# Attention row sums: GpSimd adds pairs of probability blocks before the product with ones, and the blocks lie in a ring of five units

## The reference, cut to what matters

```
Q = proj(layernorm(x), Wq, bq); K = proj(ctx, Wk, bk); V = proj(ctx, Wv, bv)
scores = einsum('bhqd,bhkd->bhqk', Q, K) / sqrt(32)
attn   = softmax(scores, axis=-1)                 # exp(s - max) / row sum
out    = einsum('bhqk,bhkd->bhqd', attn, V) @ Wo.T + bo
x = x + tanh(g_xattn) * out
x = x + tanh(g_ffn) * moe_ffn(layernorm(x))       # 8 experts, top 2, capacity 615
```

## Time and profile before

| what | value |
|---|---|
| median of the runs | 1855.63 us (1854.19 to 1856.19) |
| profiled execution | 1856.21 us |
| its span, first to last instruction | 1854.4 us |
| mean granted TensorE clock | 0.972 (1.00 in every batch of attention) |
| period of a batch in attention | 111.0 us |
| busy in one period: TensorE, VectorE, ScalarE, GpSimd | 108.7, 82.2, 56.9, 37.2 us |

### The profile page before, as it was taken

How to read it: one execution, slowest core, us unless ns; L and a number is a source line. 1 busy time by engine, 2 the same in 40 slices (tenths; PEclk the granted TensorE clock), 3 DMA queues, 4 the chain that set the end, 5 groups by cost and what they waited for, 6 DMA issues and landing times.

```text
span 1854.4 us, 29309 instructions
## 1 busy us (share of the span) xinstructions
PE 1735.9 (94%) x10322; PEld 881.9 (48%) x10322; DVE 1078.8 (58%) x2087; ACT 805.9 (43%) x1069; POOL 460.5 (25%) x424
## 2 busy tenths in 40 slices
PE   7999999999999999999814999999999999999996
PEld 4324243242423324243202767666666767676664
DVE  6777867677776777867576634435252625434331
ACT  4553735546364554735431615244252616244330
POOL 2322424223333322421211122112122122111102
PEclk9999999999999999999955999999999999999998
DMA  6333263433425433243122363626354363627301
GB/s 223 102 92 114 75 161 106 99 124 94 136 91 138 134 91 113 80 111 106 36 102 79 96 161 87 173 49 184 78 138 115 99 160 87 175 47 193 74 26 25
DMA packets 234302, 202.83 MB, mean 109 GB/s; under 512 B 141588, under 2 KB 182688, under 8 KB 230152
## 3 DMA queue, kind: packets, MB, share of 16 engines
q1 hardware_dynamic: 193288, 181.72, 33.1%
q0 software_dynamic: 40960, 20.41, 6.3%
HBM read 134.08 MB, written 43.63 MB: 96 GB/s over the span
## 4 chain that ended last, share of the span: by engine, by line
PE 82%; DVE 9%; issue 3%; ACT 3%; POOL 1%; DMA 1%; SPq 0%; DVEq 0%; ACTq 0%; POOLq 0%
PE psum L1548 22%; PE psum L1525 21%; PE psum L1353 7%; PE psum L1344 6%; PE psum L1360 6%; PE psum L1334 5%; PE psum L1324 5%; PE psum L1440 4%; PE psum L1371 3%; DVE mx L925 2%; ACT osum L792 1%; DVE reached L1076 1%; DVE x2hl L996 1%; DVE x2hl L998 1%; DVE stats L877 1%
## 5 line engine op out<-in xcount | busy, mean ns | idle before, releaser
L1548 PE MATMUL psum<-w,hT 128*123 128x512 f16 x1920 | 415.7, 379 | 0.0
L1525 PE MATMUL psum<-xgT,w 128*128 128x369 f16 (+1 forms) x3072 | 411.0, 295 | 0.8 <-DVE xgT L1177 0.8
L925 DVE TENSOR_REDUCE mx<-psum 128x1 f32<-128x512 f32 x512 | 331.2, 684 | 109.7 <-PE psum L1334 108.0
L1525 PEld LDWEIGHTS psum<-xgT,w 128*128 128x128 f16 x3072 | 298.2, 97 | 109.9 <-issue 1.9
L1548 PEld LDWEIGHTS psum<-w,hT 128*123 128x123 f16 x1920 | 259.9, 135 | 153.4
L778 ACT ACTIVATE pt<-psum 128x1024 f32<-128x1024 f32 x256 | 260.8, 1022 | 144.3 <-PE psum L1344 144.2
L851 ACT ACTIVATE h<-psum,b1c 128x369 f32<-128x369 f32 (+1 forms) x256 | 117.8, 511 | 331.6 <-PE psum L1525 331.3
L1198 DVE TENSOR_TENSOR hT<-h,hT 128x615 f16<-128x615 f32 x128 | 102.5, 801 | 212.4 <-ACT hT L854 212.4
L671 POOL DMA_INDIRECT out_dram<-y,idx_now x40 | 99.9, 2498 | 481.2 <-DVE y L1230 252.6
L1227 DVE SCALAR_TENSOR_TENSOR y<-psum,b2b 123x512 f32<-123x512 f32 x40 | 27.7, 692 | 269.5 <-PE psum L1548 269.5
L1324 PE MATMUL psum<-actT,wT 128*128 128x512 f16 x768 | 177.6, 379 | 2.0 <-DVE wT L912 2.0
(11 more groups left out here) (187 smaller groups left out, 1503.6 us busy)
## 6 DMA issues: line engine op xcount, KB each, us to landing
stage<-in_L_ffn_W_dram SPq DMA_DIRECT2D x62, 1024.0 KB, 5.3
stk<-qk_rows SPq DMA_DIRECT2D x192, 128.0 KB, 2.6
qk_rows<-qks SPq DMA_DIRECT2D x64, 256.0 KB, 2.5
xin<-in_x_dram SPq DMA_DIRECT2D x8, 1024.0 KB, 5.4
cin<-in_ctx_dram SPq DMA_DIRECT2D x8, 1024.0 KB, 7.5
xres<-in_x_dram SPq DMA_DIRECT2D x8, 1024.0 KB, 5.5
out_dram<-xres SPq DMA_DIRECT2D x32, 256.0 KB, 2.1
x_split<-x2hl SPq DMA_DIRECT2D x32, 256.0 KB, 2.3
```

Of the source, the lines that this page charges most:

```text
L925: v.reduce_max(mx[:, KT * t + qt:KT * t + qt + 1], ps, AX.X).then_inc(read, 1)
L1525: mm = t_.matmul(psum[:, (2 * m + ch) % 4, 0:(c1 - c0) * CP], w1[:, wp, kt, m * P:(m + 1) * P], xgT[:, c0:c1, KT * xp + kt, 0:CP], start=( ...
L1548: mm = t_.matmul(psum[0:CP, Y_BANK[c], :], hT[:, hp, k, c * CP:(c + 1) * CP], w2[:, wp, k, :], start=(k == 0 and (hp, wp) == (0, 0)), stop ...
```

## The change

- **Pairs on GpSimd.** The units 2p and 2p + 1 for p = 0 to 4 are added on GpSimd, in place into the first, four operations of 128x512 f32 a pair: 20 a batch. Before the pairs 0, 2 and 4 GpSimd waits for `mrow_ready` of VectorE's slots 8, 12 and 16.
- **11 products with ones.** `with_ones` now takes a term from a table: pair 0 in slot 10, pair 1 in 12, pair 2 in 14, pair 3 in 16, unit 10 in 17, unit 11 and pair 4 in 18, units 12 to 15 in 19 to 22. Slots 7, 8, 9, 11, 13 and 15 have none. A new semaphore `sums_done` counts them; `pv_done` now counts the products with values.
- **Ring of five.** `pt_units`: two units in `pt`, the other three lie over `qk32`, `x2nT` and `x2n`, which are free at that time. The exponential of unit u waits for the product with ones that used unit u - 5, and the first five for the whole of the batch before and for all of `qk_split`.
- **Two copies.** The activation of 128x1024 becomes one for bank 6 (slots 10, 14, 18) and one for bank 7 (`sums_ready`; slots 12, 16, 18).
- **Later reciprocals.** They move to the slots (15, 16, 16, 17), (17, 18, 18, 19), (19, 20, 20, 21), and `GROUP_NORM` with them from 14, 17, 20, 23 to 17, 19, 21, 23.
- **Norm of the next x.** The four `xin` operations move from GpSimd (L592) to VectorE, slots 5, 5, 6, 6. GpSimd's rstd for them moves ahead of its last two `qks` operations.

```
+PAIRS, PT_UNITS = 5, 5
+SUMS = {10: (("pair", 0),), 12: (("pair", 1),), 14: (("pair", 2),), 16: (("pair", 3),), 17: (("unit", 10),),
+        18: (("unit", 11), ("pair", 4)), 19: (("unit", 12),), 20: (("unit", 13),), 21: (("unit", 14),), 22: (("unit", 15),)}
-RECIP_SLOT = ((11, 12, 13, 14), (15, 16, 16, 17), (19, 19, 20, 20), (23, 23, 23, 23))
+RECIP_SLOT = ((15, 16, 16, 17), (17, 18, 18, 19), (19, 20, 20, 21), (23, 23, 23, 23))
+X_NORM_SLOT = (5, 5, 6, 6)
...
 # GpSimd
+                        if not last:
+                            for tt in range(KT - 1):
+                                inverse_deviation(0, tt, KT * b + (KT + tt))
                         pool.wait_ge(mrow_ready, NG * b + 1)
+                    if i == QK_FIRST + 3 and not last:
+                        inverse_deviation(0, KT - 1, KT * b + (2 * KT - 1))
...
-                pool.wait_ge(mrow_ready, NG * b + 2)
-                if not last:
-                    for tt in range(KT):
-                        ...
-                        g.tensor_scalar(xn[:, tt, :], xin[:, tt, :], mv[:, 0, tt, 0:1], rstd[:, 0, tt:tt + 1],
-                                        ALU.subtract, ALU.mult).then_inc(xn_ready, 1)
-                pool.wait_ge(mrow_ready, NG * b + 3)
+                for p in range(PAIRS):
+                    if p % 2 == 0:
+                        pool.wait_ge(mrow_ready, NG * b + (p // 2 + 2))
+                    pool.wait_ge(pv_done, UNITS * b + (2 * p + 1))
+                    for hf in range(2):
+                        copied(pool, use, ("ST", 2 * p + 1, hf), b)
+                        for j in range(2):
+                            into = pt_units[2 * p % PT_UNITS][:, hf, j, :]
+                            g.tensor_tensor(into, into, pt_units[(2 * p + 1) % PT_UNITS][:, hf, j, :],
+                                            ALU.add).then_inc(pair_added, 1)
                 pool.wait_ge(xres_in, 16 * b + 16)
...
 # ScalarE
-                            act.wait_ge(pv_done, UNITS * b + max(u - 1, 0))
+                            if u < PT_UNITS:
+                                act.wait_ge(sums_done, SUM_COUNT * b)
+                                act.wait_ge(qk_split, NQ * b + NQ)
+                            else:
+                                act.wait_ge(sums_done, SUM_COUNT * b + (sum_of_unit(u - PT_UNITS) + 1))
...
-                        s.activation(osum[:, gr % 2, :, :], psum[:, 6:8, :], ACT.Copy).then_inc(osum_ready, 1)
+                        s.activation(osum[:, gr % 2, 0, :], psum[:, 6, :], ACT.Copy).then_inc(osum_ready, 1)
+                    if t in SUMS_END[:-1]:
+                        gr = SUMS_END.index(t)
+                        act.wait_ge(sums_done, SUM_COUNT * b + (GROUP_SUMS[gr][-1] + 1))
+                        act.wait_ge(norm_done, NG * b + max(gr - 1, 0))
+                        s.activation(osum[:, gr % 2, 1, :], psum[:, 7, :], ACT.Copy).then_inc(sums_ready, 1)
...
 # VectorE
+                        for tt in range(KT):
+                            if t == X_NORM_SLOT[tt]:
+                                normalise(0, tt, KT * b + (KT + tt), xin[:, tt, :], xn[:, tt, :], xn_ready)
...
 # TensorE
+                def with_ones(s):
+                    for kind, n in SUMS.get(s, ()):
+                        i = SUM_ORDER.index((kind, n))
+                        terms = next(t for t in GROUP_SUMS if i in t)
+                        gr = GROUP_SUMS.index(terms)
+                        if i == terms[0] and gr > 0:
+                            pe.wait_ge(sums_ready, (NG - 1) * b + gr)
+                        if kind == "pair":
+                            pe.wait_ge(pair_added, 4 * PAIRS * b + (4 * n + 4))
+                        src = pt_units[(2 * n if kind == "pair" else n) % PT_UNITS]
                         for j in range(4):
-                            last = t_.matmul(psum[32 * j:32 * j + 32, 7, :], ones32[:, :],
-                                             pt[:, (2 * u + j // 2) % 4, j % 2, :], start=(kt == 0), stop=(kt == KT - 1))
-                        last.then_inc(pv_done, 1)
+                            last = t_.matmul(psum[32 * j:32 * j + 32, 7, :], ones32[:, :], src[:, j // 2, j % 2, :],
+                                             start=(i == terms[0]), stop=(i == terms[-1]))
+                        last.then_inc(sums_done, 1)
```

More of the change, by code:

```diff
@@ L51 @@
 GROUP_END = [LAG_C + 4 * g + 3 for g in range(NG)]
-RECIP_SLOT = ((11, 12, 13, 14), (15, 16, 16, 17), (19, 19, 20, 20), (23, 23, 23, 23))
+PAIRS, PT_UNITS = 5, 5
+SUMS = {10: (("pair", 0),), 12: (("pair", 1),), 14: (("pair", 2),), 16: (("pair", 3),), 17: (("unit", 10),),
+        18: (("unit", 11), ("pair", 4)), 19: (("unit", 12),), 20: (("unit", 13),), 21: (("unit", 14),), 22: (("unit", 15),)}
+SUM_ORDER = [term for slot in sorted(SUMS) for term in SUMS[slot]]
+SUM_COUNT = len(SUM_ORDER)
+GROUP_SUMS = [[i for i, (kind, n) in enumerate(SUM_ORDER) if n // (2 if kind == "pair" else 4) == g] for g in range(NG)]
+SUMS_END = [max(slot for slot in SUMS for term in SUMS[slot] if SUM_ORDER.index(term) in GROUP_SUMS[g]) for g in range(NG)]
+RECIP_SLOT = ((15, 16, 16, 17), (17, 18, 18, 19), (19, 20, 20, 21), (23, 23, 23, 23))
+X_NORM_SLOT = (5, 5, 6, 6)
 GROUP_NORM = [slots[-1] for slots in RECIP_SLOT]
@@ L58, in later_qk, with sum_of_unit @@
     return [QK_FIRST + j for j, slot in enumerate(QK_SLOT) if slot == s]
+def sum_of_unit(u):
+    return SUM_ORDER.index(("pair", u // 2) if u < 2 * PAIRS else ("unit", u))
 def later_v(s):
@@ L148, in layer_kernel @@
         pt = sb("pt", [P, 4, 2, S], f32)
+        pt_units = ([pt[:, 2 * i:2 * i + 2, :, :] for i in range(2)]
+                    + [a.rearrange("p (a b) s -> p a b s", b=2) for a in (qk32[:, :, :], x2nT[:, :, :], x2n[:, :, :])])
         mx = sb("mx", [P, H * KT], f32)
@@ L330, in layer_kernel @@
         mrow_in = [sem(f"mrow_in{g}") for g in range(NG)]
-        pv_done = sem("pv_done")
-        osum_ready, rinv_done, norm_done, a32_ready, a_hi, a_ready = (
-            sem(n) for n in ("osum_ready", "rinv_done", "norm_done", "a32_ready", "a_hi", "a_ready"))
+        pv_done, pair_added, sums_done = sem("pv_done"), sem("pair_added"), sem("sums_done")
+        osum_ready, sums_ready, rinv_done, norm_done, a32_ready, a_hi, a_ready = (
+            sem(n) for n in ("osum_ready", "sums_ready", "rinv_done", "norm_done", "a32_ready", "a_hi", "a_ready"))
         xres_biased, x1_stored = sem("xres_biased"), sem("x1_stored")
@@ L1352, in with_values @@
                             h = 4 * g + j
[L1353 to L1358 removed]
+                            last = t_.matmul(psum[32 * j:32 * j + 32, 6, :], v32[:, kt, HD * h:HD * h + HD],
+                                             pt_units[u % PT_UNITS][:, j // 2, j % 2, :], start=(kt == 0), stop=(kt == KT - 1))
+                        last.then_inc(pv_done, 1)
+                def with_ones(s):
[8 more added lines that the diff above has]
+                        src = pt_units[(2 * n if kind == "pair" else n) % PT_UNITS]
                         for j in range(4):
[L1360 to L1362 removed]
+                            last = t_.matmul(psum[32 * j:32 * j + 32, 7, :], ones32[:, :], src[:, j // 2, j % 2, :],
+                                             start=(i == terms[0]), stop=(i == terms[-1]))
+                        last.then_inc(sums_done, 1)
                 def values(tt, halves=range(2)):
@@ L1428, in batch @@
                     scores(s, 3)
-                    with_ones(s - LAG_C)
+                    with_ones(s)
                     filling(s, 1)
```

12 lines of the change are left out of this document (5 added, 7 removed).

## The result

The changed kernel takes 1874.2 us (median of 4 runs, 1871.6 to 1876.35) beside 1854.91 us (the three runs of the table above and a fourth, 1854.12 to 1856.19) of the kernel before: 1.0103 times as long, 95% interval 1.0085 to 1.012. The forecast was 1875. The profiled execution took 1875.39 us, its span 1873.6, with a mean granted clock of 0.967 in place of 0.972.

The account below looks back on a forecast made before the run. TensorE, busy 94%, bounds the kernel, but tail collisions outweigh the saving: 7 x 3.2 - 2.6 = 19.8 us on the profiled 1856.2, less 0.6, gives 1875 us. Range 1840 to 1890 us.

Parts of the forecast that it names:

- What a missing product gives back: Slots 7, 8, 9, 11, 13: maxima hold the next scores, so a slot without ones saves 0.36 us, not 1.09.
- Rival 3: Ones count in full, maxima don't hold the scores up, no collision: 1811 us; chance 0.03.
- The copies: Bank 6 copied alone takes 0.60 us, not 1.02; waits in slots 11 and 15 shrink about 0.27 us each.
- A: Start of slot 15's last score on TensorE, predicted 2.3 us earlier in a batch.
- The tail without collision: From A to the output projection: 22.3 us, before 22.6, with norms at A + 8.3 and 14.75.
- The collision: In the tail VectorE's two-input operations wait behind GpSimd's adds, 6.1 us before group 1's norm; a batch 3.2 us longer.
- Rival 1: GpSimd doesn't get in between two neighbouring `next_lo`: half the turns, 1852 us in all; chance 0.15.
- the one that asked first going first: In the tail, VectorE's two-input operations and GpSimd's SBUF-reading ones alternate by whole instructions, in order of asking.
- Rival 2: No collision: operations overlap freely or miss by chance, waits before norm 1 under 2.9 us: 1835 us; chance 0.12.
- How it reaches TensorE: ScalarE's exponentials queue behind late norms: unit 14's values at A + 23.4, not 17.6; group 2's low half ready by the projection.
- The sum: Seven batches 3.2 us longer each, the last saves 2.6: 19.8 us more in all, 1875 us.
- Costed at nothing: Pairs 0 to 3, ring of five, earlier rstd on GpSimd, norms of x on VectorE, turned inputs: no cost.

Follow-up runs that it names:

- e10: The kernel of e9 with VectorE's maxima over 256 of the 512 keys (other half left out): 1816.72 us, ratio 0.9791 to the kernel before.
- e2: Changed kernel with GpSimd's pair adds and `xres` adds cut to 8 of 512 columns, order and number kept: 1834.31 us, ratio 0.9881 to the kernel before.
- e8: Changed kernel with pair 4's four adds and the four `xres` adds replaced by memsets of an unused tensor: 1840.04 us, ratio 0.9916 to the kernel before.
- e9: Changed kernel, complete, with three `xres` adds ahead of pair 4 and `next_lo` spread over slots 16, 18, 20, 21: 1834.56 us, ratio 0.9886 to the kernel before.
- e6: Changed kernel with ScalarE's high halves of `aT` moved to slots 18, 21, 22, 23, behind the exponentials: 1864.87 us, ratio 1.0052 to the kernel before.
- e4: Kernel before with only the changed kernel's later slots for reciprocals and norms: 1855.55 us, ratio 0.9997.
- e11: Kernel before with only the next x's norms on VectorE (slots 5, 5, 6, 6) and GpSimd's rstd earlier: 1856.08 us, ratio 1.0002.
- e5: Changed kernel with three of the four `xres` adds ahead of pair 4, nothing left out: 1856.6 us, ratio 1.0005 to the kernel before.
- e1: Changed kernel with only GpSimd's pair adds cut to 8 of 512 columns, `xres` adds in full: 1844.8 us, ratio 0.9939 to the kernel before.

## Why the prediction was right

**What a missing product gives back.** Right. Score 1 starts 1.16 us behind score 3 (1.17 predicted), a slot takes 3.58 us where it took 3.94, and e10 shows that the maxima are the cause. Rival 3 falls by that. One reading behind it was off: the maximum that ends at 501.09 is the second of the four from 499.80, not the third; the 0.06 us from there to the load stand all the same.

**The copies.** The mechanism right, the size off: the waits in slots 11 and 15 vanish wholly (0.41 and 0.43 us, from the distances of `with_values`), where 0.27 each was predicted. So A comes 2.61 us earlier, not 2.3.

**The tail without collision.** e2 has the norms at A + 8.06 and 14.35 (8.3 and 14.75 predicted) and the projection at 22.35 (22.3). The last batch, without `next_lo`, shows 22.94. There `t32` of group 1 waits 1.16 us for `a32` of group 0, which stands behind the `xres` adds, and then takes 1.66 us beside the low half; the values of unit 14 come at 18.21 in place of 17.62. I had put that at nothing. GpSimd, then VectorE, last batch of the kernel after:

```profile
911.30 4.98 POOL L620 TENSOR_TENSOR xres<-xres,tgbo 128x512 f32<-128x512 f32 x4
916.38 0.69 POOL L626 TENSOR_SCALAR a<-t,bias 128x512 f32<-128x512 f32 x1
```

```profile
917.21 1.66 DVE L1008 TENSOR_TENSOR t<-osum 128x512 f32<-128x512 f32 x1 [1.16 <-POOL a L626]
```

**The collision.** Right, and e8 settles its kind. Predicted, then measured: norm of group 0 at A + 10.7, 10.56; of group 1 at 20.8, 20.17; waits before it 6.1 us, 5.9; values of unit 12 at 13.9, 13.68; of unit 14 at 23.4, 22.89. The `next_lo` beside GpSimd were put at 1.8 us and are at most 1.77. Rival 1 needed neighbours to slip through together: the pair at 572.34 and 574.02 didn't. But "the one that asked first going first" was more than the rows of the kernel before show: there a `next_lo` that starts behind `a32`'s start at 558.59 still took 0.68 us, so two neighbours did pass ahead of GpSimd once:

```profile
558.87 0.68 DVE L943 SCALAR_TENSOR_TENSOR qks<-xin,qks 128x512 f16<-128x512 f32 x1
```

The alternation is what the kernel after shows, where GpSimd has one add behind the other. The waits, as the prediction lists them one by one, sum to 6.35 us; its 6.1 is the difference of the two norms, 20.8 - 14.75. Rival 2 needed under 2.9 us of waits, and is what e2 and e9 made of the kernel.

**How it reaches TensorE.** e6 shows the one path (ScalarE's order) and the one behind it (`t32`, then GpSimd's low half, then the projection). The prediction named the first and thought the second hidden; it was, but only because the first was longer.

**The sum.** 3.2 us a batch stood for what is 2.4 us in four batches and 3.5 in three: the collision cost 0.5 us less and the copies gave 0.3 more than reckoned, and in the three the granted clock fell at a place where it cost 1.1 us, which I had not foreseen. The tails of the seven batches lose 38.7 us in all (the seven differences to 22.58) and seven savings of 2.61 are 18.3: 20.4 us, predicted 22.4. The last batch was to give 2.6 back and gave 0.9: 1.28 up to its A, as a score waited 1.1 us for its rows of `stk`, less 0.36 in the tail. The first batch reached its A only 1.07 us earlier, not 2.61: 1.5 more. Its first scores already start 1.55 us later (46.28 beside 44.73): the granted clock fell in its first projections (0.50 from 30 to 32 us), and they took 1.54 us longer than in the profiled execution before (TensorE, before and after):

```profile
28.70 10.52 PE L1324 MATMUL psum<-actT,wT 128*128 128x512 f16 x48 [1.99 <-DVE wT L912]
```

```profile
29.20 12.06 PE L1359 MATMUL psum<-actT,wT 128*128 128x512 f16 x48 [1.99 <-DVE wT L942]
```

The same fall stands in nine of the twelve profiled executions of this case (not in those of the kernel before, e8 and e9). e4 and e11, which add no pairs, have it, so it is not put down to the change. Attention so ends 20.4 - 0.9 + 1.5 = 21.0 us later, and what follows it was 1.8 us shorter, which was not traced to a cause. The span grew by 19.2 us, the median by 19.3, against 19.8. That the total lies so near is partly luck, of errors of both signs and of 1 to 2 us each; the signs and places of the steps are not.

**Costed at nothing.** e11 confirms it for the norms and the rstd. Pairs 0 to 3 are confirmed by e9, which has them in full and is level with e2. No run takes out the ring of five; e2 and e9 have it, and with 108.15 us a batch, where 108.4 was predicted, they leave it no cost that shows. From the projection to the next A the middle batches take 85.81 us in the kernel after and 85.80 in e2.

**The chances.** By the prediction's own terms "slower" adds up to 0.62 + 0.04 = 0.66, not 0.67.

## What to carry to other kernels

Work moved to an idle engine is free only if it doesn't keep out an engine that has a deadline: look at which operations of VectorE with two SBUF inputs stand on the chain at that time, and put GpSimd's reading operations elsewhere; here the same work, otherwise placed, turned a loss of 1% into a gain of 1.1%. When an engine takes its work strictly in order, a late input costs what is queued behind the waiting instruction, not the instruction itself. And removing work from the busiest engine gives back only the distance to the second limit (here 0.36 of 1.09 us a slot, up to the maxima).

## What the runs showed that was not expected

The granted clock of TensorE, 1.00 in all of attention before, falls once in the tail of each of the seven batches with `next_lo` of the kernel after, to the lower of its two levels (0.50, 1.2 GHz of 2.4), for three to four us. It follows a wait of TensorE: in four batches that of slot 19, in the other three that of slot 21. The windows of batch 3, behind the waits of slot 19 (2.05 us), and of batch 4, behind those of slot 21 (2.94 us); the clock is the third number from the end:

```profile
460.00:462.00 2.00, 0.60 (x2) 0.11 (x2) 2.00 (x2) 2.00 (x4) 2.00 (x3) 1.00 0.00 0
462.00:464.00 2.00, 1.89 (x9) 0.29 (x10) 2.00 (x4) 1.46 (x3) 1.90 (x2) 0.61 0.00 0
464.00:466.00 2.00, 2.00 (x10) 0.20 (x8) 2.00 (x3) 1.02 (x1) 1.75 (x2) 0.54 0.00 0
466.00:468.00 2.00, 2.00 (x16) 0.39 (x12) 2.00 (x4) 0.00 (x0) 0.00 (x0) 1.00 0.15 29
...
584.00:586.00 2.00, 1.60 (x10) 0.19 (x8) 1.80 (x3) 1.52 (x2) 0.42 (x1) 0.83 1.04 197
586.00:588.00 2.00, 2.00 (x14) 0.33 (x10) 0.00 (x0) 0.74 (x1) 0.69 (x1) 0.50 1.00 186
```

In the first place the slow work ends before the late exponentials of unit 14, and costs nothing (values of unit 13 at A + 18.33 in place of 16.75, those of unit 14 unmoved); in the second it costs 1.1 us. In e5 it fell in three of seven batches after the same 2.05 us in slot 19, in e6 in five of seven after 2.4 us, at some 1.6 and 1.7 us each; in the tails of e1, with waits of 1.42 us in slot 19, and of e2 and e9 it never fell. What decides between batches alike in every start is open; so an error of some us remains in any forecast of a kernel with such waits.

Two smaller things: an add of 128x512 f32 on GpSimd takes 1.24 us alone, and 1.41 (pair 4 of e9) to 1.58 us (`xres` of the kernel after) on the mean of four beside VectorE's two-input operations; and moving the norms by one to three slots, alone, cost 0.0 us (e4), though ScalarE's wait for them is in the trace.
